# Causal score matmuls in two 64-column strips, with half of the token tiles loaded and stored half-swapped

## What is computed

```
phi(x)  = exp(x @ omega - 0.5 * sum(x*x)) / sqrt(m)
phi_q, phi_k = phi(q * scale), phi(k * scale)        # (b, h, t, 128)
S   = cumsum_t(phi_k[..., :, None] * v[..., None, :])
Z   = cumsum_t(phi_k)
y   = (phi_q . S) / (phi_q . Z + eps)                # causal: key tokens s <= query token t
x   = x + ga * (y @ W_proj + b_proj)
```

## Time and profile before

| | |
|---|---|
| median of 3 runs | 839.67 us (836.02 to 840.61) |
| profiled execution, its own time | 835.22 us |
| its span in the trace | 833.4 us |
| PE busy | 765.5 us (92%) |
| DVE busy | 546.9 us (66%) |
| ACT busy | 410.9 us (49%) |
| mean granted clock of PE | 0.984 |

### The profile page before, as it was taken

The page is one execution under the profiler, slowest core; times in us unless marked ns, Lnnn a source line. Parts: engine busy times, 40 slices in busy tenths (PEclk is TensorE's granted clock), DMA queues, the critical chain, the costliest instruction groups (busy, mean ns, idle before and its releaser), DMA issues.

```text
span 833.4 us, 16957 instructions
## 1 busy us (share of the span) xinstructions
PE 765.5 (92%) x6138; PEld 603.4 (72%) x6138; DVE 546.9 (66%) x1289; ACT 410.9 (49%) x758; POOL 47.0 (6%) x62
## 2 busy tenths in 40 slices
PE   2989998999899999999999998999999998999596
PEld 2767767876698766977678765987678776887366
DVE  5546666776667775776666766677656766665456
ACT  2365545564456444654455544564446543555122
POOL 1101000010001000010000100010000100010000
PEclk9979999999999999999999999999999999999989
DMA  8680072203702064111722037020731017110000
GB/s 271 149 196 2 24 207 57 76 0 94 189 0 75 0 194 89 43 32 42 195 45 75 0 103 180 0 75 0 202 81 57 18 50 200 33 52 1 1 1 26
DMA packets 46540, 65.37 MB, mean 78 GB/s; under 512 B 8716, under 2 KB 22840, under 8 KB 46392
## 3 DMA queue, kind: packets, MB, share of 16 engines
q1 hardware_dynamic: 46520, 65.10, 29.0%
HBM read 39.87 MB, written 25.17 MB: 78 GB/s over the span
## 4 chain that ended last, share of the span: by engine, by line
PE 73%; DVE 14%; DMA 7%; issue 3%; ACT 2%; SPq 1%; DVEq 0%; POOL 0%; ACTq 0%
PE pa L513 11%; PE prod L528 7%; DMA qk_parts<-qk_l 6%; PE ring L492 6%; PE pa L379 5%; PE pa L381 4%; PE pa L380 4%; PE prod L547 4%; PE pa L619 4%; PE ring L379 4%; PE ring L497 3%; PE ring L380 3%; PE ring L381 3%; PE prod L513 2%; PE ring L695 2%
## 5 line engine op out<-in xcount | busy, mean ns | idle before, releaser
L513 PE MATMUL pa<-phq,phkT 128*128 128x128 f32 x896 | 115.1, 276 | 0.0
L513 PEld LDWEIGHTS pa<-phq,phkT 128*128 128x128 f32 x896 | 107.8, 191 | 2.3 <-issue 1.6
L820 ACT ACTIVATE phq<-ring 128x512 f32<-128x512 f32 x96 | 58.9, 614 | 90.6 <-PE ring L492 89.7
L1077 DVE TENSOR_TENSOR am_phk<-pa,const 128x512 f32<-128x512 f32 x112 | 74.2, 685 | 32.0 <-PE pa L513 32.0
L1230 DVE SCALAR_TENSOR_TENSOR am_phk<-ring,am_phk 128x512 f32<-128x512 f32 x64 | 44.2, 691 | 55.4 <-PE ring L695 55.4
L379 PE MATMUL pa<-wo_r,qk_r 128*128 128x256 f32 x256 | 72.1, 282 | 0.6 <-DVE qk_l L1235 0.6
L381 PE MATMUL pa<-wo_l,qk_r 128*128 128x256 f32 x256 | 72.1, 282 | 0.0
L380 PE MATMUL pa<-wo_r,qk_l 128*128 128x256 f32 x256 | 71.8, 281 | 0.0
L882 ACT ACTIVATE qk_r<-phq 128x512 fp32r<-128x512 f32 x64 | 40.5, 632 | 63.3 <-DVE phq L1239 62.8
L528 PE MATMUL prod<-am_phk,v_ones 128*32 128x256 f32 x1024 | 61.9, 382 | 4.6 <-DVE tg L1108 4.6
L379 PE MATMUL ring<-h_r,wi_r 128*128 128x512 f32 x128 | 57.7, 451 | 3.6 <-DVE am_phk L1230 2.9
(11 more groups left out here) (189 smaller groups left out, 1566.2 us busy)
## 6 DMA issues: line engine op xcount, KB each, us to landing
xq<-qk_parts SPq DMA_DIRECT2D x48, 512.0 KB
qk_parts<-qk_r SPq DMA_DIRECT2D x32, 256.0 KB, 3.3
qk_parts<-qk_l SPq DMA_DIRECT2D x32, 256.0 KB, 3.6
tok<-in_L_attn_x SPq DMA_DIRECT2D x8, 512.0 KB, 4.6
xr<-in_L_attn_x SPq DMA_DIRECT2D x8, 512.0 KB, 3.7
out_x<-tg SPq DMA_DIRECT2D x16, 256.0 KB, 2.2
norm_parts<-norm_r SPq DMA_DIRECT2D x16, 128.0 KB, 3.5
norm_parts<-norm_l SPq DMA_DIRECT2D x16, 128.0 KB, 5.1
```

The source lines that it names most:

```text
L513: mm = pe.matmul(score_bank(q, a)[:, tt], phkT[:, q % 2, a, tt], phq[:, q // 2 % 2, 2 * (q % 2) + a, tt], start=True, stop=True)
L820: act.activation(dst, src, ACT.Exp).then_inc(exp_done.sem, 1)
L1077: dve.tensor_tensor(am[:, 2 * (q % 2) + a, :].rearrange("p (c t) -> p c t", c=NT), score_bank(q, a)[:].rearrange("p (c t) -> p c t", c=NT) ...
```

## The change

`scores` issues two matmuls per chunk in place of one. The first has the chunk's first 64 key positions as its stationary operand and writes PSUM partitions 0 to 63, the second the last 64 and partitions 64 to 127. For `q` of 2 and up one of the two moves only 64 of the 128 query positions: the quarter in which every key is later than every query isn't computed. Its place in PSUM keeps positive numbers from the whole groups of `q` = 0 and 1, and the mask makes them zero.

For the two strips to have the same work, the quarter left out lies in strip 1 for even chunks and in strip 0 for odd ones. To that end odd chunks hold their tokens in another order: tokens 64 to 127 in partitions 0 to 63 and tokens 0 to 63 in partitions 64 to 127. The mask gets a second half for that order, and DVE's minimum runs over it in two pairs of chunks (the same 512 elements). Each load of `tok` and `xr` becomes three DMAs (`swapped`), as does each store.

```
-CONSTS = {"ident": P, "causal": P, "headsum": VA, "prio": E}
+CONSTS = {"ident": P, "causal": 2 * P, "headsum": VA, "prio": E}
...
+            def swapped(tile, rows):
+
+                return ((tile[:, 0::2], rows[:, 0::2]), (tile[0:HP, 1::2], rows[HP:P, 1::2]),
+                        (tile[HP:P, 1::2], rows[0:HP, 1::2]))
...
-            load(ld_x, (tok[:], x_rows[0]))
+            load(ld_x, *swapped(tok[:], x_rows[0]))
...
-                    sp.dma_start(dst[:, 2 * b:2 * b + 2, :],
-                                 tg[:, b, :].rearrange("p (t c) -> p t c", t=2)).then_inc(out_done.sem, 16)
+                    for tile, rows in swapped(tg[:, b, :].rearrange("p (t c) -> p t c", t=2),
+                                              dst[:, 2 * b:2 * b + 2, :]):
+                        sp.dma_start(rows, tile).then_inc(out_done.sem, 16)
...
-                sp.dma_start(tok[:], block_rows(x_rows, i + 1)).then_inc(x_loaded.sem, 16)
+                load(x_loaded, *swapped(tok[:], block_rows(x_rows, i + 1)))
...
                 for c in range(NT):
-                    tt = slice(c * P, (c + 1) * P)
-                    mm = pe.matmul(score_bank(q, a)[:, tt], phkT[:, q % 2, a, tt],
-                                   phq[:, q // 2 % 2, 2 * (q % 2) + a, tt], start=True, stop=True)
+                    for strip in range(2):
+                        first = c * P + strip * HP
+                        whole = q < 2 or strip == c % 2
+                        tt = slice(c * P, (c + 1) * P) if whole else slice(first, first + HP)
+                        mm = pe.matmul(score_bank(q, a)[strip * HP:(strip + 1) * HP, tt],
+                                       phkT[:, q % 2, a, first:first + HP],
+                                       phq[:, q // 2 % 2, 2 * (q % 2) + a, tt], start=True, stop=True)
                 mm.then_inc(a_ps.sem, 1)
...
-                                  over_tiles(causal, NT), ALU.min).then_inc(am_done.sem, 1)
+                                  over_tiles(causal, NT // 2), ALU.min).then_inc(am_done.sem, 1)
...
-    causal = np.where(r[:, None] <= r[None, :], np.finfo(np.float32).max, 0).astype(np.float32)
+    orders = r, (r + HP) % P
+    causal = np.concatenate([np.where(o[:, None] <= o[None, :], np.finfo(np.float32).max, 0) for o in orders], 1)
```

More of the change, by code:

```diff
@@ L61 @@
 TILES = 6
+HP = P // 2
+ROW_MOVES = 3
 PAD = -3.0e38
@@ L226, in build @@
         late_pe, late_vec, late_act = sig("late_pe"), sig("late_vec"), sig("late_act")
-        x_loaded, tok_free = sig("x_loaded", 16), sig("tok_free", 1)
+        x_loaded, tok_free = sig("x_loaded", 16 * ROW_MOVES), sig("tok_free", 1)
         ln1_vec, ln1_pool, hn_ready = sig("ln1_vec", 10), sig("ln1_pool", 2), sig("hn_ready", 4)
@@ L249, in build @@
         yT_ps, yT_done, prj_ps = sig("yT_ps", 2), sig("yT_done", 2), sig("prj_ps", 2)
-        xr_loaded, xr_biased, x2_step = sig("xr_loaded", 16), sig("xr_biased", 1), sig("x2_step", 2)
+        xr_loaded, xr_biased, x2_step = sig("xr_loaded", 16 * ROW_MOVES), sig("xr_biased", 1), sig("x2_step", 2)
         ln2_vec, ln2_pool = sig("ln2_vec", 10), sig("ln2_pool", 2)
@@ L262, in build @@
         scaled = sig("scaled", NT)
-        out_done = sig("out_done", 32)
+        out_done = sig("out_done", 2 * 16 * ROW_MOVES)
         x_rows = x.rearrange("b (n t p) c -> (b n) p t c", p=P, t=NT)
@@ L358, in ffn_stores @@
                     wait(sp, fin, n, b + 1)
-                    sp.dma_start(dst[:, 2 * b:2 * b + 2, :],
-                                 tg[:, b, :].rearrange("p (t c) -> p t c", t=2)).then_inc(out_done.sem, 16)
+                    for tile, rows in swapped(tg[:, b, :].rearrange("p (t c) -> p t c", t=2),
+                                              dst[:, 2 * b:2 * b + 2, :]):
+                        sp.dma_start(rows, tile).then_inc(out_done.sem, 16)
             front_moves(0)
-            sp.dma_start(xr[:], x_rows[0]).then_inc(xr_loaded.sem, 16)
+            load(xr_loaded, *swapped(xr[:], x_rows[0]))
             with sp.Fori(0, NB - 1) as i:
                 wait(sp, tok_free, i, 1)
-                sp.dma_start(tok[:], block_rows(x_rows, i + 1)).then_inc(x_loaded.sem, 16)
+                load(x_loaded, *swapped(tok[:], block_rows(x_rows, i + 1)))
                 front_moves(i + 1)
                 ffn_stores(i)
-                sp.dma_start(xr[:], block_rows(x_rows, i + 1)).then_inc(xr_loaded.sem, 16)
+                load(xr_loaded, *swapped(xr[:], block_rows(x_rows, i + 1)))
             ffn_stores(NB - 1)
@@ L1007, in ln1_stats @@
                 if first:
-                    dve.wait_ge(ld_x.sem, 16)
+                    dve.wait_ge(ld_x.sem, 16 * ROW_MOVES)
                 else:
-                    wait(dve, x_loaded, n - 1, 16)
+                    wait(dve, x_loaded, n - 1, x_loaded.per)
                 for t in range(NT):
@@ L1076, in causal_scores @@
                 wait(dve, a_ps, n, 2 * q + a + 1)
-                dve.tensor_tensor(am[:, 2 * (q % 2) + a, :].rearrange("p (c t) -> p c t", c=NT),
-                                  score_bank(q, a)[:].rearrange("p (c t) -> p c t", c=NT),
-                                  over_tiles(causal, NT), ALU.min).then_inc(am_done.sem, 1)
+                dve.tensor_tensor(am[:, 2 * (q % 2) + a, :].rearrange("p (c t) -> p c t", c=NT // 2),
+                                  score_bank(q, a)[:].rearrange("p (c t) -> p c t", c=NT // 2),
+                                  over_tiles(causal, NT // 2), ALU.min).then_inc(am_done.sem, 1)
             def advance_state(n, gr):
@@ L1346, in residual @@
             def residual(n):
-                wait(pool, xr_loaded, n, 16)
+                wait(pool, xr_loaded, n, xr_loaded.per)
                 wait(pool, mod2_set, n, 1)
@@ L1370, in constants @@
     ident = np.eye(P, dtype=np.float32)
-    causal = np.where(r[:, None] <= r[None, :], np.finfo(np.float32).max, 0).astype(np.float32)
+    orders = r, (r + HP) % P
+    causal = np.concatenate([np.where(o[:, None] <= o[None, :], np.finfo(np.float32).max, 0) for o in orders], 1)
+    causal = causal.astype(np.float32)
     headsum = np.zeros((P, VA), np.float32)
```

## The result

| | before | after |
|---|---|---|
| median | 840.14 us (4 runs) | 861.50 us (4 runs, 861.09 to 862.01) |
| ratio (of the means) | | 1.0266, 95% interval 1.0238 to 1.0295 |
| profiled execution: span | 833.4 us | 859.6 us |
| PE busy | 765.5 us | 773.3 us |

The account below looks back on a forecast made before the run. PE was taken as the bound (92% busy, 73% of the chain). Eight blocks of +0.30 (+2.4) and DMAs of +1.5 and +0.5 made +4.4 us on the median of 839.67: 844.1 us, range 840.5 to 853.0.

Parts of the forecast that it names:

- Rival 2: Scores: nothing is saved, a group stays at 0.89 us and layouts are paid in full; 861 us, chance 0.07.
- the groups did shrink to 0.66: Score groups of q 2 and up: two independent strips take 0.66 us against 0.89, -0.23 a group.
- Inside the loop nothing: DMAs in the block loop: the extra issues cost nothing, since the tok load still lands before DVE reads it.
- The prices of the layouts: PE's layout changes: 0.15 us into two strips, 0.20 back to tiles; +0.97 ahead of a block's first products.
- Rival 1: Scores: strips wait for each other in program order, a single group takes 0.77 us; 849.7 us, chance 0.28.
- Rival 3: Scores: two 64-column strips need no drain, so layout changes cost nothing; 832.9 us, faster, chance 0.07.
- Along the block: One block's sum: products of groups 0 to 3 at +0.97, +0.73, +0.66, +0.30 us, so +0.30 a block.
- `scores(2, 0)` ends at +0.89, and with it DVE's mask and the running state: Head group 0: scores, DVE's mask and running state all come 0.89 us later than before, after products at +0.97.
- The DMAs: Split loads and stores: +0.5 us at the start, +1.5 at the end, nothing inside the loop.
- The issue price: Each DMA issue on SP was taken as 0.4 to 0.5 us, 0.47 for the six stores at the end.

Follow-up runs that it names:

- before_shift64: The kernel before with 64 empty instructions at PE's start, ahead of its loop, and nothing else changed; 864.9 us in one run.
- after_unrolled: The changed kernel with PE's seven blocks written out instead of looped, other engines keeping their loops; 850.8 us, 1.0129 times before.
- before_shift128: The kernel before with 128 empty instructions at PE's start, ahead of its loop; 843.0 us in one run.
- before_unrolled: The kernel before with PE's seven blocks written out instead of looped; 837.0 us, 0.9988 times before.

## Why the prediction was wrong

**The step that failed is one that was never priced.** The change was costed by the time of its matmuls. Rival 2 had "the program issues slower" in one clause, as a price on each group of scores, and its 861 us fell on the measured time by chance: the groups did shrink to 0.66, and the largest part of the loss lies where there is no score at all. The forecast's "Inside the loop nothing" was said of the DMAs alone; the return from block to block stood in the sum at zero, without a reason. It cost six waits of 2.0 us, 12 us in all. What the front showed and the sum left out is the count: eight matmuls for four, in 16 groups, 64 matmuls of four instructions each, in the body of a loop that is branched back to. `before_shift64` shows the mechanism without anything of the change, and `after_unrolled` takes it out: 9 to 11 us of the 21.4 by the medians, 12 by the six gaps in the trace.

**The prices of the layouts were right.** Last matmul of the block at 157.02, so its end at about 157.14; first products at 166.10: 8.96. Before it was 153.56 to 159.56, 6.00. Take off the fetch (2.11 between the end and the scores, less the 0.10 that the change of layout holds anyway, 2.01) and +0.95 is left; the forecast was +0.97.

**Rival 1 fell.** `scores(2, 0)` runs from 168.63 to the transposes at 169.45, 0.82: 0.66 and the 0.15 of a first half load and a drain. With strips waiting for each other it would be 0.93. Two narrow windows of PE's timeline show the strips running freely; up to 168.75, and in the group's second half:

```profile
168.63 0.34 PE L524 MATMUL pa<-phq,phkT 128*64 128x128 f32 x3
```

```profile
168.79 0.73 PE L524 MATMUL pa<-phq,phkT 128*64 128x128 f32 x13
```

By 168.75 three records had started; the next starts at 168.79. In program order the first strip's second long record stands ahead of both short ones of the other strip. In the trace both short ones have started by 168.74, at 168.63 and 168.74, and the next two, at 168.79 and 168.80, are long. The Trainium skill, page "TensorE: Matmul & The Clock Gate", section "Part 3: Packing small matmuls", says that matmuls start and end in program order. For the starts of matmuls in different column strips this trace is against it. The pair of groups ahead of the reads takes 171.53 - 170.03 = 1.50, by the sum 1.47.

**Rival 3 fell** with the same rows: every excursion shows its 0.10 on the way out.

**Along the block** the forecast gave back 0.24, 0.07 and 0.36 in head groups 0, 1 and 2. Products to products it was 10.67, 11.77 and 9.38, before 10.72, 11.70 and 9.62: -0.05, +0.07 and -0.24. So a block loses 0.95 - 0.22 = 0.73 by its layouts and not 0.30. In the last block the three steps are 10.51, 10.51 and 9.11, before 10.72, 10.73 and 9.43, so it gives back 0.75 and loses 0.20. That makes 5.3 us in all and not 2.4. The term that was mis-sized is in group 0, "`scores(2, 0)` ends at +0.89, and with it DVE's mask and the running state". The mask did come as forecast, 169.56 - 166.10 = 3.46 after the products, where it was 3.53. But the state did not come with it. DVE's timeline, after:

```profile
169.56 0.69 DVE L1089 TENSOR_TENSOR am_phk<-pa,const 128x512 f32<-128x512 f32 x1 [0.77 <-PE pa L524]
170.39 0.23 DVE L1101 COPY s_sb<-state 128x128 f32 x1
...
173.02 0.68 DVE L1109 TENSOR_TENSOR s_sb<-prod_sb,prod 128x512 f32<-128x512 f32 x1
```

And the state's copy before:

```profile
163.78 0.23 DVE L1089 COPY s_sb<-state 128x128 f32 x1
```

It starts 170.39 - 166.10 = 4.29 after the products, and 4.22 before (163.78 - 159.56): +0.07, with the state transposes (3.35 and 3.33 after the products at their start, and one longer first step) and not with the mask. By the program the copy waits for the transposes (`wait(dve, d_ps, n, gr + 1)`) and stands behind the mask. Before, both came together: the mask ended at 163.78, and 163.78 is 0.89 after the transposes' start, as 170.39 is 0.94 after it now. It had waited for the transposes all along; the mask's end hid it. I read a chain off the row that stood in front, not off what the row waited for. L1109 and the output transposes follow (7.65 after the products, forecast 7.52), and PE's saving in the pair of groups is lost to DVE in group 0 too, not only in group 1.

**The DMAs**: forecast +2.0, measured +4.1 on the median (1.7 to 6.9), and 3.5 in the traces: 1.6 at the start, forecast 0.5, and 1.9 at the end, forecast 1.5. The issue price was from DMAs of 128 partitions; three issues in a row of the split load took 0.64 each, the six stores 0.56 each.

**The sum as it stands now**: six returns 12, layouts 5.3, DMAs 4.1: 21.4 us, and the medians differ by 21.4. That it comes out to the tenth is luck, since the DMAs' term alone is known to no better than 2.6 either way.

The traces differ by 26.2, which is more. The rest lies behind the last products. The windows of the last block, after: busy us and counts of PE, PEld, DVE, ACT, POOL, then PE's granted clock and the DMAs.

```profile
791.60:797.60 6.00, 4.03 (x68) 2.09 (x68) 2.56 (x7) 0.60 (x1) 0.00 (x0) 0.96 0.01 3
797.60:803.60 6.00, 4.04 (x14) 3.12 (x15) 1.05 (x4) 1.19 (x2) 0.00 (x0) 0.50 0.00 0
```

The same stretches before:

```profile
771.40:777.40 6.00, 4.03 (x68) 2.09 (x68) 2.53 (x7) 0.60 (x1) 0.00 (x0) 1.00 0.01 3
777.40:783.40 6.00, 3.96 (x22) 3.26 (x23) 1.19 (x5) 1.09 (x2) 0.00 (x0) 1.00 0.00 0
```

The last block has no next front to fill its gaps, and PE's clock falls to its lower level, 1.2 GHz (0.50), in the stretch after group 3's products. In the trace of before it falls later. The change isn't needed for that: `before_shift64` and the kernel with halved matmuls have before's stores and no strips, and both take 66.4 us from the last block's group 3 products to the end, not 62.0. `before_shift128` and `before_unrolled`, whose PE loop isn't fetched again, take 61.9 both. Whether the waits of the loop bring the clock down earlier at its end, or it is chance, five executions can't tell. So about 4 of the 26.2 us are that, and the profiled execution of before is one of its quick ones: 835.2 against a median of 840.1.

## What to carry to other kernels

Where a change multiplies instructions inside a loop, count the body in code pages of 256 and look at the instruction queue's packets in the profile: many more of them than the program is long means that the loop is read again at each return. Writing out the hot engine's loop costs a line and takes that away; so does moving a body that can fit into seven code pages, if the empty instructions hide behind another wait. A layout change on PE costs about 0.35 us there and back; strips pay next to strips, not as islands of 0.9 us among whole-array work. And a saving on one engine is worth what the other engine's row really waited for, not what stood in front of it.

## What the runs showed of the hardware that I had not expected

- The same PE loop is kept on the chip or fetched again by its place alone: 13 packets and 839 us, or 67 packets and 865 us, with 64 empty instructions between the two. 54 packets more in six returns is nine a return.
- A matmul in one column strip can start ahead of one that stands before it in the program in the other strip (168.74 against 168.79): 384 columns a strip take 0.66 us, with unequal lengths.
- Three issues of split loads took 1.93 us on SP, 0.64 each, where whole ones took 0.47; an empty instruction on PE with a semaphore took 0.15 us.
